# Language-model tower on one core: low halves of both recurrent layers issued ahead of both high halves, with respaced background pieces and a reordered start

## What is computed

```python
# token module: embedding, grouped causal conv over 2 taps, relu, projection 128 -> 64
embed = table[y]; x = conv1d(embed, conv_w, groups=16); out = einsum(relu(x), proj_w) + proj_b
# then layer norm over the 64 features; then a two-layer tanh RNN, hidden 256, batch 8, 1024 steps
def step(h, p_t):
    h = jnp.tanh(p_t + h @ W_hh.T); return (h, h)
h = _rnn_layer(x, W_ih_0, W_hh_0, b_ih_0, b_hh_0)
h = _rnn_layer(h, W_ih_1, W_hh_1, b_ih_1, b_hh_1)
y = h @ fc_w.T + fc_b          # with a residual and a layer norm behind it
```

## Time and profile before

| | us |
|---|---|
| median of three runs (1385.34 to 1390.23) | 1386.47 |
| the profiled execution, its own time | 1385.33 |
| its span in the profile | 1383.5 |
| start, up to the first low-half matmul | 52.6 |
| recurrence | to about 897 |
| stages behind it | about 487 |

### The profile page before, as it was taken

One profiled execution on the slowest core, in us unless ns is written; L12 is line 12 of the kernel. 1 busy time (PEld: TensorE's weight loads), 2 busy tenths in 40 slices (PEclk: granted clock), 3 DMA queues, 4 the chain that ended last, 5 costly groups with the idle time before them and its releaser, 6 DMA issues.

```text
span 1383.5 us, 64463 instructions
## 1 busy us (share of the span) xinstructions
PE 1209.8 (87%) x27009; PEld 998.9 (72%) x27009; DVE 814.0 (59%) x3407; ACT 828.9 (60%) x4697; POOL 108.8 (8%) x162
## 2 busy tenths in 40 slices
PE   2599999998999999999999999884666884799998
PEld 1499999998999998999999999822225873233332
DVE  5555565665565565556556555456782554677775
ACT  1366666666666666666666766563557661456554
POOL 2300000000000000000000000000110111111010
PEclk9555555555555555555555555587777996899999
DMA  5001000000001000000000000000000000000000
GB/s 153 6 4 20 4 4 19 5 5 19 4 5 20 5 4 19 5 4 5 4 5 4 4 5 4 4 16 1 0 0 0 1 0 0 1 15 8 15 8 15
DMA packets 21563, 14.52 MB, mean 10 GB/s; under 512 B 10737, under 2 KB 20529, under 8 KB 21297
## 3 DMA queue, kind: packets, MB, share of 16 engines
q1 hardware_dynamic: 21296, 10.69, 3.5%
HBM read 8.55 MB, written 2.13 MB: 8 GB/s over the span
## 4 chain that ended last, share of the span: by engine, by line
PE 62%; issue 32%; DVE 2%; POOL 2%; DMA 1%; ACT 0%; POOLq 0%; SPq 0%; DVEq 0%; ACTq 0%
PE bank L577 38%; PE bank L666 6%; PE bank L652 4%; PE bank L429 3%; PE bank L437 2%; PE bank L508 2%; PE bank L647 2%; POOL stat L322 1%; PE bank L661 1%; PE bank L1366 1%; PE bank L383 1%; PE bank L1180 1%; DMA space<-in_x 1%; PE bank L1376 0%; DVE space L696 0%
## 5 line engine op out<-in xcount | busy, mean ns | idle before, releaser
L577 PE MATMUL bank<-space,whh_hi 128*128 128x8 f16 x16384 | 614.9, 170 | 13.8 <-issue 7.8
L577 PEld LDWEIGHTS bank<-space,whh_hi 128*128 128x128 f16 x16384 | 550.3, 106 | 38.0 <-issue 8.1
L696 DVE TENSOR_TENSOR space<-h_f,space 128x16 f16<-128x16 f32 x2048 | 356.5, 176 | 359.4 <-ACT h_f L677 317.1
L677 ACT ACTIVATE h_f<-bank 128x16 f32<-128x16 f32 x2048 | 377.8, 184 | 274.7 <-PE bank L577 262.6
L683 ACT ACTIVATE space<-bank 128x16 f16<-128x16 f32 x2048 | 376.8, 184 | 11.4 <-PE bank L577 11.4
L666 PE MATMUL bank<-space,wih_hi 128*128 128x32 f16 x2048 | 178.3, 188 | 2.6 <-issue 2.6
L577 PE MATMUL bank<-space,whh_lo 128*128 128x32 f16 (+2 forms) x2192 | 147.6, 189 | 0.0
L429 PE MATMUL bank<-onehot,tab 128*128 128x128 f16 x448 | 120.0, 268 | 4.8 <-DVE onehot L414 4.8
L652 PE MATMUL bank<-xr,wih_lo 128*128 128x32 f16 x512 | 123.4, 241 | 0.0
L1180 PE MATMUL bank<-xt,wx 128*128 (+1 forms) x352 | 110.0, 407 | 11.0 <-ACT xt L334 11.0
L666 PEld LDWEIGHTS bank<-space,wih_hi 128*128 128x128 f16 x2048 | 114.2, 104 | 2.7 <-issue 2.7
(11 more groups left out here) (252 smaller groups left out, 1672.3 us busy)
## 6 DMA issues: line engine op xcount, KB each, us to landing
space<-in_x SPq DMA_DIRECT2D x7, 516.0 KB, 9.0
out<-res SPq DMA_DIRECT2D x8, 256.0 KB, 2.6
space<-in_wrec SPq DMA_DIRECT2D x1, 768.0 KB, 9.8
space<-in_wx SPq DMA_DIRECT2D x1, 740.5 KB, 11.6
space<-in_x SPq DMA_DIRECT2D x1, 512.0 KB, 9.9
brec<-in_brec SPq DMA_DIRECT2D x1, 512.0 KB, 4.5
space<-router_dram SPq DMA_DIRECT2D x8, 64.0 KB, 2.3
ew<-in_ew SPq DMA_DIRECT2D x1, 256.0 KB, 3.9
```

The source lines that it names most:

```text
L577: mm = pe.matmul(own[:, m, :], w[:, k, m * P:(m + 1) * P], steps(h, k), start=False, stop=False, skip_group_check=True)
L677: act.activation(h_f[layer][:, s % 2, :, :], own, ACT.Tanh, scale=scale[layer]).then_inc(s_h[layer], 1)
L696: dve.tensor_tensor(h[layer][:, :, s % RINGS[layer], 1, :], h_f[layer][:, s % 2, :, :], h[layer][:, :, s % RINGS[layer], 0, :], ALU.subtra ...
```

## The change

Six things are changed together.

1. On PE and ACT the four groups of a slot run low 0, low 1, high 0, high 1. DVE's two subtractions keep their order.
2. The background pieces are respaced (`LEAD` 33 for 6, all offsets new): each slot gets at most one DVE operation of a piece, the 12 output matmuls stand one a slot (one slot has two), and the projection is done with float16 halves: six 64-column matmuls in three slots for two float32 ones; ACT and DVE make the halves of the relu.
3. The norms have fewer DVE instructions: the division of the mean goes into the centring, that of the variance into ACT's square, and the epsilon to a second POOL instruction in `root`.
4. Layer 0 keeps 128 steps in its ring, not 32.
5. Token ids after the first block are loaded piece by piece, 28 DMAs of 129 KB for seven of 516 KB; the first block is the first DMA of all.
6. The start: biases are loaded to 65 partitions and split before the recurrent weights' scales are known; of the weights only layer 0's are split ahead of the first norm; layer 1's follow behind it; the maxima and the scaling of the wide weights move into slots of the recurrence. Slots with negative numbers (`lead_in`) run ahead of and between the steps of the first norm.

```diff
-RINGS = (32, 256)
+RINGS = (128, 256)
...
-PERIOD, LEAD = 32, 6
+PERIOD, LEAD = 32, 33
+ROWS = 65
...
-            [(vid[:, :], a["vid"]), (embt[:, :], a["embt"]), (wconv[:, :, :], a["wconv"])],
+            [(vid[:, :], a["vid"]), (embt[:, :], a["embt"]), (wconv[:, :, :], a["wconv"]), (wproj[:, :], a["wproj"])],
+            [(brec[0:ROWS, :, :].rearrange("p a h -> p (a h)"), a["brec"].partition_broadcast(ROWS)),
+             (bsum[0:ROWS, B_O:B_O + 2 * D], a["bov"].partition_broadcast(ROWS))],
             [(wrec[:, :, :, :], a["wrec"]), (wfc[:, :, :], a["wfc"]), (wih0[:, :], a["wih0"]),
-             (wproj[:, :], a["wproj"]), (bproj[:, :], a["proj_b"].partition_broadcast(P)),
-             (fcb[:, :], a["fc_b"].partition_broadcast(P)), (eye16[:, :], a["eye16"]),
-             (brec[:, :, :].rearrange("p a h -> p (a h)"), a["brec"].partition_broadcast(P)),
-             (bsum[:, B_O:B_O + 2 * D], a["bov"].partition_broadcast(P))],
+             (bproj[:, :], a["proj_b"].partition_broadcast(P)),
+             (fcb[:, :], a["fc_b"].partition_broadcast(P)), (eye16[:, :], a["eye16"])],
...
         def mean_of(dve, link, r):
 
             link(dve.reduce_sum(r.stat[:, 0, :], r.cur[:, :, :], AX.X))
-            link(dve.tensor_scalar(r.stat[:, 1, :], r.stat[:, 0, :], 1.0 / D, None, ALU.mult))
 
         def centre(dve, r, g):
 
-            dve.tensor_tensor(r.xc[:, :, :], r.cur[:, :, :], r.each(1), ALU.subtract).then_inc(g.centred, 1)
+            dve.scalar_tensor_tensor(r.xc[:, :, :], r.each(0), -1.0 / D, r.cur[:, :, :], ALU.mult,
+                                     ALU.add).then_inc(g.centred, 1)
 
         def square(act, r, g, k):
 
             act.wait_ge(g.centred, k + 1)
-            act.activation(r.sq[:, :, :], r.xc[:, :, :], ACT.Square).then_inc(g.squared, 1)
-
-        def variance(dve, link, r, g, k):
+            act.activation(r.sq[:, :, :], r.xc[:, :, :], ACT.Square, scale=D ** -0.5).then_inc(g.squared, 1)
+
+        def variance(dve, r, g, k):
 
             dve.wait_ge(g.squared, k + 1)
-            link(dve.reduce_sum(r.stat[:, 2, :], r.sq[:, :, :], AX.X))
-            dve.tensor_scalar(r.stat[:, 3, :], r.stat[:, 2, :], 1.0 / D, EPS, ALU.mult, ALU.add).then_inc(g.variance, 1)
-
-        def root(pool, r, g, k):
+            dve.reduce_sum(r.stat[:, 2, :], r.sq[:, :, :], AX.X).then_inc(g.variance, 1)
+
+        def root(pool, link, r, g, k):
 
             pool.wait_ge(g.variance, k + 1)
+            link(pool.tensor_scalar(r.stat[:, 3, :], r.stat[:, 2, :], EPS, None, ALU.add))
...
-            if 4 <= o < 20:
-                b, n = (o - 4) // 8, (o - 4) % 8
+            if 4 <= o < 12 or 14 <= o < 22:
+                b, n = (o - 4) // 10, (o - 4) % 10
                 v, tap, part = n // 4, n // 2 % 2, n % 2
                 if o == 4:
                     pe.wait_ge(s_oh, m + 2)
+                elif o == 14 and m:
                     pe.wait_ge(prep.copied, m + 2)
                 mm = pe.matmul(P_CONV[:, b * P:(b + 1) * P], tab[part][:, v, tap, :],
                                onehot[:, m % 2, v, b, tap:tap + P], start=(n == 0), stop=(n == 7),
                                skip_group_check=True)
-                if o == 19:
+                if o == 21:
                     mm.then_inc(s_conv, 1)
-            elif o in (22, 23):
-                b = o - 22
-                pe.wait_ge(s_relu, 2 * m + 4)
-                mm = pe.matmul(P_PROJ[:, b * D:(b + 1) * D], relu[:, b, :], wproj[:, :], start=True, stop=True,
-                               skip_group_check=True)
-                if b == 1:
+            elif 24 <= o < 27:
+                pe.wait_ge(s_relo, m + 3)
+                for c in (2 * (o - 24), 2 * (o - 24) + 1):
+                    mm = project(pe, P_PROJ, [x[:, c // 3, :] for x in relu], c // 3, c % 3)
+                if o == 26:
                     mm.then_inc(s_proj, 1)
-            elif o == 33:
+            elif o == 44:
...
+        def project(pe, own, x, b, c):
+
+            part, w = ((0, 0), (0, 1), (1, 0))[c]
+            return pe.matmul(own[:, b * D:(b + 1) * D], x[part], wproj16[w][:, :], start=(c == 0), stop=(c == 2),
+                             skip_group_check=True)
...
-            if 24 <= o < 30:
-                if o == 24:
+            turns = (54, 55, 59, 60, 60, 61, 62, 63, 64, 65, 66, 67)
+            if o in turns:
+                if o == turns[0]:
                     pe.wait_ge(s_lo[1], OPEN + (j + 1) * UNIT)
-                for c in (2 * (o - 24), 2 * (o - 24) + 1):
+                for c in range(turns.index(o), turns.index(o) + turns.count(o)):
                     mm = output(pe, O_SUM, c // 6, j, b0 + c // 6, c % 6)
-                if o == 29:
+                if o == turns[-1]:
                     mm.then_inc(s_fc, 1)
-            elif o == 43:
+            elif o == 77:
...
             low(0, g - LATE)
+            low(1, g - OFF - LATE)
             high(0, g)
-            low(1, g - OFF - LATE)
             high(1, g - OFF)
...
         def rec_scalar(act, g, scale):
-            for layer in range(2):
-                for part, s in ((1, g - layer * OFF - LATE), (0, g - layer * OFF)):
+            for part in (1, 0):
+                for layer in range(2):
+                    s = g - layer * OFF - part * LATE
                     if not 0 <= s < T:
...
+            if k == 1 and 0 <= o < 12:
+                wide_most(dve, link, o)
+            elif k == 1 and o == 20:
+                scales(dve, link, S_FF1, S_END, 3, 0)
+            elif k == 2 and o < 20 and o % 10 != 5:
+                wide_weights(dve, link, o - (o > 5) - (o > 15))
...
+            def some_ids(sp, m):
+
+                j, b0 = place(m + 4)
+                sp.dma_start(ids[:, m % 4, :, :],
+                             a["x"][b0:b0 + 2, j * UNIT - 1:(j + 1) * UNIT].partition_broadcast(P)).then_inc(
+                                 s_ids[m % 4], 16)
+
...
+                if g == 2:
+                    for m in range(4):
+                        some_ids(sp, m)
+            for m in range(4, SUBS):
+                sp.wait_ge(s_oh, m - 2)
+                some_ids(sp, m)
...
+            pool.wait_ge(s_w[1], 16 * len(loads[1]))
+            for l in range(2):
+                link(pool.tensor_tensor(bsum[0:ROWS, l * H:(l + 1) * H], brec[0:ROWS, 2 * l, :],
+                                        brec[0:ROWS, 2 * l + 1, :], ALU.add))
...
-            pool.partition_all_reduce(stat[:, 6, 3:4], stat[:, 5, 3:4], P, RMAX).then_inc(s_mxa, 1)
+            pool.partition_all_reduce(stat[:, 6, 3:5], stat[:, 5, 3:5], P, RMAX).then_inc(s_mxa, 1)
+            split_rows(0, 2 * H + 2 * D)
             pool.wait_ge(s_mx, 2)
             pool.partition_all_reduce(stat[:, 6, 0:3], stat[:, 5, 0:3], P, RMAX).then_inc(s_mxa, 1)
...
+            lead_in(pe, rec_tensor, -45, -9)
...
+            lead_in(dve, lambda e, g: rec_vector(e, link, g), -50, -12)
+            link(split(whh_hi[0][:, :, :], whh_lo[0][:, :, :], wrec[:, 0, :, :], S_L0))
+            split(wih0_hi[:, :], wih0_lo[:, :], wih0[:, :], S_L0).then_inc(s_prep, 1)
...
+            link(split(wih1_hi[:, :, :], wih1_lo[:, :, :], wrec[:, 1, :, :], S_L1))
+            link(split(whh_hi[1][:, :, :], whh_lo[1][:, :, :], wrec[:, 2, :, :], S_L1))
+            split(wfc_hi[:, :, :], wfc_lo[:, :, :], wfc[:, :, :], S_FC).then_inc(s_prep1, 1)```

The first place is PE in mid-recurrence, one whole slot with the projection's matmuls around it (`wproj`, `relu`: the projection; `state0_low` is the semaphore of layer 0's low half, and so on). Before:

```order
L666 MATMUL bank<-space,wih_hi 128x32 x4
L437 MATMUL bank<-wproj,relu 128x64 [waits conv_relu]
L577 MATMUL bank<-space,whh_hi 128x8 [waits state0_low]
L577 MATMUL bank<-space,whh_hi 128x8 x3
L577 MATMUL bank<-space,whh_hi 128x8 [waits state0_high]
L577 MATMUL bank<-space,whh_hi 128x8 x3
L577 MATMUL bank<-space,whh_hi 128x8 [waits state1_low]
L577 MATMUL bank<-space,whh_hi 128x8 x3
L577 MATMUL bank<-space,whh_hi 128x8 [waits state1_high]
```

285 lines of the change are left out of this document (151 added, 134 removed).

## The result

The changed kernel takes **1362.72 us** (median of four runs, 1360.74 to 1363.39), the kernel before 1385.90 (four runs, 1384.82 to 1390.23). The ratio is 0.9825, with a 95% interval from 0.9801 to 0.9848. That is faster, but by 23 us where 49 were forecast, and it lies outside the range. The profiled execution took 1363.29 us with a span of 1361.3.

A forecast was written before the change was run, and what follows sets the result against it. A slot's floor was taken as layer 0's 0.75 us loop through PE, ACT and DVE, lengthened by PE work above its room. 33 + 12 + 4.5 - 1 = 48.5 us off 1385.33 gave 1337 us, range 1322 to 1353.

The forecast's parts named there:

- the start (6): Before the first low-half slot: earlier ids and reordered splits bring it to about 48 us for 52.63; 4.5 us gained.
- The respaced pieces (2, 3, 4): Recurrence slots: PE work above the slots' room falls from 1.81 to 0.63 us a period; 33 us over 28 pieces.
- The new order (1): Slot's groups on PE and ACT: the floor doesn't move; worth 0, bounds -0.02 to +0.02 us a slot.
- the rival in which DVE doesn't overlap the two: Slot's two DVE subtractions: the second waits for an empty pipe, PE stands 0.07 us each slot; 1372 us, chance 0.05.
- The ids (5): Recurrence, 100 to 600 us: smaller id loads remove gaps where PE's instruction fetch stands behind loads; 12 us, bounds 0 and 12.
- The rival of the remaining gaps: Token id loads: each small load still holds the fetch, 28 gaps of 0.4 to 1.3 us; 1349 to 1373 us, chance 0.08.
- The clock: PE in the recurrence: forecast stays at 0.50 (1.2 GHz); rival has it rise to 2.4 GHz, 1269 us, chance 0.03.
- POOL's root: Norms' root in the recurrence: addition and power each load code at 1.64 us, missing the slot; about 1480 us, chance 0.03.
- Behind the recurrence: Stages behind 897 us: should keep their 487 us within a few us; more would be a change of clock.

The follow-up runs named there:

- Late waits: Changed kernel with the wait for a piece's DVE operation written directly ahead of the instruction that reads its result, one slot later: 1354.90 us, ratio 0.9770.
- The fours: Changed kernel with token ids of four pieces, four DMAs of 129 KB, issued one behind the other every fourth piece: 1378.91 us, ratio 0.9936.

## Why the prediction was wrong, and where it was right

**The failed step is the start (6).** It took "a change of code as the 1.64 us gap at 28.12". That figure is the piece of a change that was left on the chain after DVE's work had covered the rest; the change itself was 8.08 us (29.75, `<-issue`, above). A residual of the chain is what a cost adds *there*, not the cost. Putting the additions ahead of the first reduction uncovered one change of 10.4 us, and putting the split between the reductions set two more of 6.6 and 5.6 where DVE waits. The three are 22.6 us of the chain, for 4.3 us in the kernel before. Two experiments show it from both sides: with the reductions first the start is 14.2 us shorter, and one multiplication in the kernel before makes it 10.9 us longer. The order of POOL, as quoted ahead of the prediction, has loads as ISA rows without tiles at L961 and L971; I named one of them in the sum and priced it wrongly, and the one ahead of the first reduction has no term at all.

The remaining part of the term was too high too. With the reductions first the start is 52.74 us, no gain on 52.63. The ids as first DMA brought 0.2 us for the forecast's 1.4, since DVE waits for the whole first group of loads, to which the change adds `wproj`:

```profile
11.84 0.06 DVE L1483 MEMSET embt<- 128x1 f32 x1 [11.84 <-DMA wproj<-in_wproj]
```

DVE didn't reach the second reduction 4 us earlier either: with the reductions first it stands at 22.34 us, for 21.30 before. And the roots start at 40.75 us even then, behind all of the split, for 39.43 before. From there to the first low-half slot it is 12.0 us for 13.2, where I had counted 7 fewer: layer 1's splits and the norm of the next piece stand there now. The 4.5 us can't be added up again from the terms that the forecast lists: 8.2 + 1.64 - 4 is 5.8 and not 5, and the half splits have no price of their own. That half of the splits stand ahead of the first norm brings nothing as long as the norm waits for POOL.

**The respaced pieces (2, 3, 4): the mechanism is right, the term was mis-sized.** I forecast 1.18 us a period and 33 us. The period went from 25.97 to 24.95, 1.02 us, and 28 pieces make 29. The largest part, the float32 projection, was sized well: put back, it costs 20 us where I had 0.67 x 28 = 19. What is missing is the second wait at the subtraction. In the trace of before I read it as work, "slots with two DVE operations of a piece ... some 0.07 late", and took it for gone with the respacing. But the subtraction of 602.63 in the earlier trace rows is itself one of the 112 with a semaphore instruction ahead of it (at 602.56). It stayed, since it hangs on an operation followed by a wait, not on two operations in a slot. Late waits bring the period to 24.72; the forecast had 24.79. So the wait is more than the 0.16 us a period that were missing, and the work above the room was put a little too high.

**The new order (1) is right at 0:** 1363.02 us without it. Quiet slots stay at 0.754. The second subtraction starts 0.11 us or less behind the first, so the rival in which DVE doesn't overlap the two is out.

**The ids (5) are right.** The five long slots of before are 16.2 us long in all, 4.0 by their positions' medians, so they cost 12.2; in the changed kernel there are none. That PE's instruction fetch is what stands still in them, as the forecast took it, no run shows directly. The rival of the remaining gaps is out. The fours show that what is queued together matters.

**The clock** granted is 0.50 (1.2 GHz) throughout the recurrence, also at 794 busy of 796 us, as forecast. The Trainium skill's page "TensorE: Matmul & The Clock Gate" (Why this matters for your kernels) advises to keep TensorE busy to have the full clock. Over these 796 us the trace does not show that.

**POOL's root** (the slower rival) loads no code between its two instructions:

```profile
64.11 0.23 POOL L367 TENSOR_SCALAR prepare_stat<-prepare_stat 128x2 f32<-128x2 f32 x1 [3.68 <-DVE prepare_stat L362]
64.43 0.73 POOL L368 TENSOR_TENSOR prepare_stat<-prepare_stat,nhalf 128x2 f32<-128x2 f32 x1
```

It takes 1.05 us from start to end for the 0.69 of the earlier trace rows. The code-change cost that I had given this rival at 1.64 us was real and larger, but it fell at the start, where I hadn't put a case for it.

**Behind the recurrence** the changed kernel shows 3.8 us more. The same code took between 490.6 and 500.9 us in the traces of the kernels above, at granted clocks of 0.87 and 0.84:

```profile
833.48:1324.10 490.62, 372.25 (x2226) 189.73 (x2226) 309.05 (x674) 260.54 (x385) 52.02 (x39) 0.87 0.03 6
```

```profile
856.29:1357.20 500.91, 382.70 (x2226) 198.21 (x2226) 308.99 (x674) 260.22 (x385) 52.01 (x39) 0.84 0.02 6
```

The kernel before lies between them, 494.2 us at 0.86, and so does the changed one, 497.9 at 0.85. They differ by execution, so I count these 3.8 us neither for nor against the change. The sum of the misses is 18.8 + 3.7 + 3.8 = 26.3 of 26.3 us.

## What to carry to other kernels

Price a cost that you are about to uncover by the idle time of its own engine, not by what the chain of waits shows of it, and count how often an engine changes between kinds of work that need other code. In a loop that is closed by one short instruction, give that instruction one wait only (look for a semaphore instruction ahead of it in the trace), and write waits that belong to side work in front of what uses it. Spread loads that nobody is in a hurry for: behind 516 KB queued together PE stood still here, though it waited for nothing that the profile shows.
